# Oscillator front: input rows normalised in two halves, bias and decay products on GpSimd, TensorE's first waits moved to its first convolution

## What is computed

```python
x = x + retention(layernorm(x))      # 4 layers
x = x + ffn(layernorm(x))            # shared expert + one routed expert of 8 for each row
x = x + oscillator(layernorm(x))
x = x + ffn(layernorm(x))
```

```python
xc = causal_conv1d(x, conv_w, 4 taps, per channel) + conv_b
qk = xc @ qk_w.T;  q = k = qk / max(norm(qk per head), 1e-12)
v, g = xc @ v_w.T, sigmoid(xc @ g_w.T + g_b)
state = (v * cos(t * freqs) + v * shift(k)) * g
decay = gamma ** t
mem = cumsum(state * decay, over t) / (decay + 1e-6)
out = (mem * q) @ o_w.T
out = (out - mean) / sqrt(var + 1e-5) * ln_g + ln_b
```

## Time and profile before

| | us |
|---|---|
| median of 3 runs | 592.39 |
| the runs | 590.1, 592.39, 597.42 |
| the profiled execution | 590.93, of which the profile's span is 589.1 |

### The profile page before, as it was taken

The page is one execution under the profiler, slowest core; times in us unless marked ns, Lnnn a source line. Parts: engine busy times, 40 slices in busy tenths (PEclk is TensorE's granted clock), DMA queues, the critical chain, the costliest instruction groups (busy, mean ns, idle before and its releaser), DMA issues. The chain is left out here.

```text
span 589.1 us, 13981 instructions
## 1 busy us (share of the span) xinstructions
PE 523.4 (89%) x4372; PEld 409.7 (70%) x4372; DVE 495.6 (84%) x1824; ACT 362.3 (61%) x830; POOL 214.1 (36%) x223
## 2 busy tenths in 40 slices
PE   0788999999999999999968896996499999897994
PEld 0656787878888888888856564994255777456992
DVE  6799999999999999999978897788958999993653
ACT  2577888787888887887747594686144310132760
POOL 2343543543543543543530073474200000072661
PEclk9899999999999999999999999899699999998998
DMA  8979999993000000000000311323000000012315
GB/s 305 364 201 187 182 171 183 181 177 59 3 1 2 2 3 2 2 2 2 2 1 2 116 47 54 87 65 104 0 0 1 2 0 2 0 52 59 101 56 160
DMA packets 61129, 43.29 MB, mean 73 GB/s; under 512 B 4640, under 2 KB 58272, under 8 KB 60800
## 3 DMA queue, kind: packets, MB, share of 16 engines
q1 hardware_dynamic: 56160, 35.42, 30.7%
q0 software_dynamic: 2496, 5.13, 2.6%
q10 hardware_dynamic: 2400, 1.84, 1.0%
HBM read 18.38 MB, written 24.01 MB: 72 GB/s over the span
## 5 line engine op out<-in xcount | busy, mean ns | idle before, releaser
L544 POOL TENSOR_TENSOR qk<-cosq,sinq 128x512 f32<-128x512 f32 x32 | 44.0, 1376 | 164.2 <-DVE cosq L865 164.2
L524 POOL TENSOR_TENSOR att<-att,small 128x512 f32<-128x512 f32 x63 | 79.0, 1275 | 10.2 <-ACT att L360 10.1
L368 ACT ACTIVATE xz<-resid,nmr,rs 128x128 f32<-128x128 f32 x128 | 53.1, 482 | 15.5 <-DVE nmr L921 15.4
L1234 POOL DMA_INDIRECT rows_back<-ffn_yt,ffn_front x46 | 47.8, 1038 | 40.5 <-DVE ffn_yt L1585 36.5
L1414 PE MATMUL banks<-ffn_xtT,ffn_wt 128*128 128x128 f32 x368 | 51.6, 286 | 2.0 <-DVE ffn_hr L1579 2.0
L1414 PEld LDWEIGHTS banks<-ffn_xtT,ffn_wt 128*128 128x128 f32 x368 | 47.1, 200 | 2.8 <-ACT ffn_wt L1261 2.2
L809 DVE TENSOR_TENSOR att<-banks,small 128x512 f32<-128x512 f32 x64 | 43.9, 685 | 4.9 <-PE banks L583 3.9
L1086 PE MATMUL banks<-small 128*128 128x512 f32 (+1 forms) x74 | 31.7, 547 | 13.6 <-POOL osc_taps L1657 11.5
L1225 POOL DMA_INDIRECT rows_in<-ffn_front,ffn_slot x32 | 31.9, 998 | 29.0 <-DVE ffn_slot L1497 20.5
L1217 POOL MEMSET ffn_all_one<- 128x8 f32 x2 | 0.2, 104 | 107.6 <-POOLq L1649 83.8
L360 ACT ACTIVATE att<-banks 128x512 f32<-128x512 f32 x63 | 37.9, 603 | 0.5 <-PE banks L583 0.5
(11 more groups left out here) (259 smaller groups left out, 1430.5 us busy)
## 6 DMA issues: line engine op xcount, KB each, us to landing
rows_in<-zero_rows SPq DMA_DIRECT2D x16, 1032.0 KB, 19.2
shared_tab<-in_rot SPq DMA_DIRECT2D x3, 1024.0 KB, 12.5
routed_sb<-in_routed SPq DMA_DIRECT2D x1, 3072.0 KB, 12.4
ffn_front<-rows_in SPq DMA_DIRECT2D x46, 64.5 KB, 1.8
ffn_yg<-rows_back SPq DMA_DIRECT2D x8, 256.0 KB, 3.7
shared_tab<-in_rot ACTq DMA_DIRECT2D x1, 1024.0 KB, 10.0
w<-in_W SPq DMA_DIRECT2D x2, 512.0 KB, 7.4
times<-in_times SPq DMA_DIRECT2D x1, 1024.0 KB, 4.9
```

The source lines that it names most:

```text
L368: ins = act.activation(xz[:, n], resid[:, (g % GROUPS) * 2 + n % 2], ACT.Identity, scale=rs[:, n:n + 1], bias=nmr[:, n:n + 1])
L524: pool.tensor_tensor(att[:, c, HALF:HEADS], att[:, c, HALF:HEADS], spread(causal.unsqueeze(1), 1, HALF), ALU.mult) \
L544: pool.tensor_tensor(qk[:, v].rearrange("p a b c -> p (a b c)"), cosq[:].rearrange("p a b -> p (a b)"), sinq[:].rearrange("p a b -> p (a b ...
L1234: pool.indirect_dma_start(rows_back, bass.IndirectOffsetOnAxis(ap=token, axis=0), yt[:, j % RING], None).then_inc(stored[j % RING], 16)
```

## The change

Five things are edited:

- ffn, both calls: `shared_add` of the last block goes ahead of the loop over the four pieces; only the last piece waits for it. In ffn(0) only the first two pieces' `bn_stats` are still taken there.
- oscillator, DVE: the statistics of chunks 8 to 15 are taken between the chain instructions of the first half's rsqrt; `standardised(0)` and `(1)` follow, then aggregation, chain and `standardised(2)`, `(3)` for the second half. The reciprocal of `token_decays` becomes `token_quotients`, inside the second chain.
- `biased` and `decayed` go from DVE to GpSimd, behind the taps, `decayed` as two instructions of 128x512.
- PE: the waits for taps and constants go from the start of its list to `convolution(0)`; 3 dummy matmuls in place of 4; `convolution(1)` goes right behind `convolution(0)`, and `transposes(2)` and `(3)` to behind `gates(0)` and `queries_keys(1)`.
- ACT: `convolved(1)` directly behind `convolved(0)`; `transposed(2)` and `(3)` later.

```diff
@@ ffn, DVE
+                shared_add(LATE)
                 for b in range(NCH // BLK):
-                    if b == 2:
-                        shared_add(LATE)
+                    if b == LATE:
                         dve.wait_ge(s["shared_added"], LATE + 1)
...
-                    if call == 0:
+                    if call == 0 and b < 2:
@@ oscillator, GpSimd
+                def biased(b):
+                    part = x[:, 4 * b:4 * b + 4]
+                    pool.wait_ge(s["xn_ready"], 4 * b + 4)
+                    pool.tensor_tensor(part, part, spread(w["ln_b"][:].unsqueeze(1), 1, 4), ALU.add) \
+                        .then_inc(s["bias_added"], 1)
+
+                def decayed(b):
+                    blk_t = slice(W * b, W * b + W)
+                    for f in range(HALF):
+                        ins = pool.tensor_tensor(cos[:, f, blk_t], cos[:, f, blk_t], dec[:, f, blk_t], ALU.mult)
+                    ins.then_inc(s["cos_ready"], 1)
+
+                for b in range(NB):
+                    decayed(b)
+                    biased(b)
@@ oscillator, PE
-                pe.wait_ge(s["taps_ready"], 4)
-                pe.wait_ge(s["edges"], 2)
-
                 def convolution(b):
+                    if b == 0:
+                        pe.wait_ge(s["taps_ready"], 4)
+                        pe.wait_ge(s["edges"], 2)
@@ oscillator, DVE
+                def input_scales(h):
+                    part = slice(8 * h, 8 * h + 8)
+                    for c in range(8 * h, 8 * h + 8):
+                        ins = dve.bn_aggr(mv[:, c], stats[:, c])
+                    ins.then_inc(s["stats_chain"], 1)
+                    dve.wait_ge(s["stats_chain"], 9 * h + 1)
+                    dve.tensor_scalar(var[:, part], mv[:, part, 1], EPS, None, ALU.add).then_inc(s["rs_chain"], 1)
+                    yield
+                    at = (RL + 1) * h
+                    dve.wait_ge(s["rs_chain"], at + 1)
+                    yield from rsqrt_steps(dve, var[:, part], vy[:, part], vt[:, part], s["rs_chain"], at + 1,
+                                           s["rs_ready"], rs[:, part])
+                    dve.wait_ge(s["rs_ready"], h + 1)
...
+                first_half, second_half = input_scales(0), input_scales(1)
+                for c in range(8, NCH):
+                    next(first_half)
+                    dve.bn_stats(stats[:, c], x[:, c]).then_inc(s["stats_chain"], 1)
+                rest(first_half)
                 standardised(0)
                 standardised(1)
-                biased(0)
-                decayed(0)
+                dve.wait_ge(s["stats_chain"], 9)
+                links(second_half, 4)
+                tables.token_quotients(dve)
+                rest(second_half)
                 standardised(2)
                 standardised(3)
-                decayed(1)
-                biased(1)
                 head_sums(0)
-                links(in_head[0], 2)
-                decayed(2)
-                links(in_head[0], 3)
-                biased(2)
-                links(in_head[0], 1)
-                decayed(3)
                 rest(in_head[0])
                 head_sums(1)
                 keys(0)
                 links(in_head[1], 2)
                 queries(0)
-                biased(3)
```

More of the change, by code:

```diff
@@ L150, in build @@
                 ffn_sems, tables, None)
-        oscillator(nc, a, xin, stats, eye, small, banks, ow, tabs, ffn_sems)
+        oscillator(nc, a, xin, stats, eye, small, banks, ow, tabs, ffn_sems, tables)
         ffn(nc, 1, xin, stats, ffn_w, rows_in, rows_back, token_ids, eye, small, route, banks, loaded_ffn,
@@ L1607, in _, with oscillator @@
                             dve.bn_stats(stats[:, c], x[:, c])
-def oscillator(nc, a, x, stats, eye, small, banks, w, tabs, ffn_sems):
+def oscillator(nc, a, x, stats, eye, small, banks, w, tabs, ffn_sems, tables):
     NB, W = 4, T // 4
@@ L1704, in _ @@
                 convolved(0)
-                transposed(2)
+                convolved(1)
                 squares(0)
                 copied(0)
-                transposed(3)
-                convolved(1)
+                transposed(2)
                 squares(1)
                 copied(1)
+                transposed(3)
                 gate(0)
@@ L1831, in scaled @@
                     projected(b, SCALED, w["o_g"], s["scaled_ready"])
-                keep_running(pe, banks[:, 4, :], small, 4)
+                keep_running(pe, banks[:, 4, :], small, 3)
                 transposes(0)
@@ L1836, in _ @@
                 convolution(0)
+                convolution(1)
+                queries_keys(0)
+                gates(0)
                 transposes(2)
+                queries_keys(1)
                 transposes(3)
[L1839 to L1842, removed]
                 cosine(0)
@@ L1893, in standardised @@
                                           ALU.subtract, ALU.mult).then_inc(s["xn_ready"], 1)
[L1895 to L1904, removed]
                 def gated(b):
@@ L1918, in summed @@
                 def summed(b):
+                    if b == 0:
+                        dve.wait_ge(s["edges"], 2)
                     dve.wait_ge(s["keyed"], b + 1)
@@ L2257, in token_decays, with token_quotients @@
         dve.tensor_tensor(key[:], key[:], spread(row[:, 0].unsqueeze(1), 1, NCH), ALU.mult)
-        dve.reciprocal(out[:], out[:])
+    def token_quotients(self, dve):
+        self.link(dve, dve.reciprocal(self.out_dec[:], self.out_dec[:]))
     def out_weights(self, dve):
```

2 lines of the change are left out of this document (1 added, 1 removed).

## The result

| | kernel before | changed kernel |
|---|---|---|
| median of 20 runs, us | 592.54 (590.1 to 597.42) | 597.26 (591.14 to 602.98) |
| ratio | 1 | 1.0064 [1.0046, 1.0083] |
| profiled execution / span, us | 590.93 / 589.1 | 592.73 / 590.9 |

The changed kernel is slower by 0.64%, 3.8 us; 3.8 us less had been forecast. By the 2% measure it is the same, but it moved the other way, out of the range. The ratio leaves out three slow executions of the changed kernel (600.66 to 602.98 us); the medians, which have them in, lie 4.7 us apart.

A forecast was written before the change was run, and what follows sets the result against it. DVE bounds the border, then taps and PE up to cosine(0). Convolution gain 7.1 less 1.1 hold and 2.2 waiting gives 3.8 us: 590.93 to 587.1 profiled, forecast 587.9 from the middle of known times; range 584.8 to 592.0.

The forecast's parts named there:

- Border: From ffn(0) into the oscillator: with reciprocal and eight statistics moved, the oscillator starts at 414.2, 3.1 us earlier.
- DVE's first chain: Oscillator front: aggregation and chain with statistics in its gaps give scales at 417.45 undisturbed, from a start at 414.2.
- the 1.1 us set aside for it: Allowance before the first convolution for GpSimd's products holding a DVE chain step; bounds 0 and 2.9 us.
- What GpSimd does to DVE: Oscillator front: GpSimd's products may hold two-input chain steps, cutting the first convolution's gain from 7.1 to 6.0 us.
- The rival with its place and number of products (five): Before transposes(1), five products hold the normalisations 6.2 us; convolution at 426.2, kernel 593 us; chance 0.05.
- PE's new front: Oscillator start to first convolution: three dummies end about when the rows come, at either clock; undisturbed convolution at 420.0.
- the rival with PE at 1.2 GHz: First convolutions: four to eight passes at the lower clock cost 1.7 to 3.4 us; kernel 590.4 us; chance 0.12.
- the 4.9 from which the prediction called its front a loss: Oscillator front: hold in us at which the front's 7.1 gain less the new 2.2 wait is used up.
- Convolution to `cosine(0)`: Same 13.2 us of PE work plus 2.2 waiting for ACT's fourth copy; cosine(0) at 436.5, 3.8 us earlier.
- DVE in time: Second chain and head sums: DVE ready near 439, gated product waits for PE until 443.6; zero cost taken.
- End of the kernel: In ffn(1), shared_add makes piece one 0.3 us late, but the last additions wait for DMA: effect 0.
- Range: Whole kernel: eight in ten medians from 584.8 (no hold, lowest run) to 592.0 us (clock or overrun, middle).

The follow-up runs named there:

- last-copy-first kernel: Changed kernel with biased and decayed back on DVE, PE's transposes(3) before queries_keys(1) and ACT's transposed(3) before squares(1): ratio 0.9898, again 0.9902.
- in the second: The changed kernel itself, unaltered, profiled and measured again: ratio 1.0041 against the kernel before.
- the one with PE's waits back: Changed kernel with PE's waits for taps and constants back at the start of its list and four dummy matmuls instead of three: ratio 1.0000 against the changed kernel.

## Why the prediction was wrong

- **Border**: 3.1 us forecast, 3.2 measured. Right, by ffn(0)'s length; the start itself came at 415.18, not 414.2, since retention was 1.0 longer.
- **DVE's first chain**: scales 3.25 us after the start forecast, 3.2 measured (415.18 to 418.38). Right; the last chain step slipped in ahead of GpSimd's product, so the 1.1 us set aside for it was not paid there.
- **What GpSimd does to DVE**: the step that failed. It looked for the hold only in two-input instructions, took 1.1 us for it with a bound of 2.9, and let the normalisations pass because they read one tensor. They were held for 4.7 us; the first convolution came 11.0 us after the start, where 6.9 was forecast. The rival with its place and number of products (five) was written down, and given 5%. That its convolution time (426.2) was met to 0.01 us is luck: the start came 1.0 later than forecast, and only 4.7 of its 6.2 us were paid. What the prediction quoted beside it from the Trainium skill's "SBUF — State Buffer", Who interferes with whom, that `tensor_scalar` can take both ports, pointed the right way. And "no row shows such an instruction held" was wrong: the kernel before has one, a `tensor_scalar` that reads one SBUF tensor, beside GpSimd's taps (418.08 to 420.43) and again in ffn(1) with GpSimd idle:

```profile
418.78 0.28 DVE L159 TENSOR_SCALAR osc_vy<-osc_var 128x16 int32<-128x16 int32 x1
...
505.64 0.17 DVE L159 TENSOR_SCALAR ffn_vy<-ffn_var 128x16 int32<-128x16 int32 x1
```

- **PE's new front**: that the dummies end with the rows was right only if the rows were on time. With the rows held PE idled 3.25 us, and the clock cost 1.0 us in the convolutions: the rival with PE at 1.2 GHz came on top of the one with the held normalisations. Hold and clock together, 5.7 us, are over the 4.9 from which the prediction called its front a loss; the hold alone is just under it.
- **Convolution to `cosine(0)`**: 13.2 + 2.2 us of waiting for ACT. The wait measured 2.17. Right, and taken away in the last-copy-first kernel.
- **DVE in time**: the gated product waited 4.51 us for PE in the changed kernel. Right, although the second eight normalisations were held too (5.03 us) and ended at 437.0.
- **End of the kernel**: ffn(1) was taken as unchanged. In the first profile it was (84.3 for 84.9), in the second it took 91.2. The prediction had no term for a clock that falls in a later stage in some executions. The oscillator and the border explain 1.4 of the measured 3.8 us; that the other 2.4 are this clock is argued from two profiles and the mean clocks.
- **Range**: its lower end by its own terms is 590.1 - 5.1 = 585.0, not 584.8. Nothing hangs on it.

Open: what makes the fall in ffn(1) last 3.4 us in one execution and 20.5 in another, and why the changed kernel meets the long one so much more often than the one with PE's waits back.

## What to carry to other kernels

Before work is given to GpSimd, look at what DVE runs beside it. Here a `tensor_scalar` on SBUF was stopped by every kind of GpSimd instruction tried, a two-input one by those that read; beside two-input products the hold lasted up to the whole product, so that a chain of 0.2 us steps ran at GpSimd's pace. Give GpSimd the time in which DVE reduces or aggregates, or leave the work on DVE where DVE has idle time. A wait that is moved later on PE gains nothing if what follows waits for someone else, and a burst of dummies followed by a pause can leave PE with the lower clock just when the real work comes.

## What the runs showed of the hardware

- DVE's `tensor_scalar` of 128x128 with its scalars read from SBUF takes 0.34 us undisturbed, more than the 0.29 of one of 128x256 in the kernel before (L2256), so its time shows no higher rate. It is held all the same: it takes up to 1.31 us beside products, 0.67 to 1.02 beside one memset, and up to 0.70 beside a one-input instruction of 1.48.
- `bn_aggr` (eight of them) and `tensor_reduce` on SBUF kept their length beside GpSimd's products: 0.63 and 1.22 us. `reciprocal` never ran beside a product; beside a one-input instruction of GpSimd it kept its 1.74.
- The same program's last stage took 84.3 or 91.2 us, by how long PE's clock stayed at 1.2 GHz (3.4 or 20.5 us) after one fall at the same place.
